# Reordering all five engines of a fused tokenizer, attention and channel-mix kernel, with other PSUM banks

## What is computed

```python
h = _L0_tok_ref(x, ln1_g, ln1_b, W, b, ln2_g, ln2_b)        # (64, 196, 256)
h = jnp.concatenate([h, txt], axis=1)                        # (64, 273, 256)
h = h + attn(_layernorm(h))
h = h + ffn(_layernorm(h))

# attn: heads attend to each other inside one token (the tensors are (n, s, head, d))
scores = jnp.einsum('nqhd,nkhd->nhqk', Q, K) * scale         # Q, K, V: 16 heads of 16
out = jnp.einsum('nhql,nlhd->nqhd', softmax(scores), V) @ Wo.T + bo
# ffn
x_prev = concatenate([zeros, x[:, :-1]]);  xr, xk = mixes of x and x_prev by mu_r, mu_k
r = sigmoid(xr @ W_r.T);  k = square(relu(xk @ W_k.T));  return r * (k @ W_v.T)
```

## Time and profile before

| | us |
|---|---|
| three runs | 1718.64, 1730.68, 1731.56 (median 1730.68) |
| the profiled execution, its time | 1723.9 |
| its span from first to last instruction | 1722.2 |
| TensorE busy | 1481.2 (86%) |
| VectorE busy | 1323.2 (77%) |
| ScalarE busy | 1260.7 (73%) |
| GpSimd busy | 933.9 (54%) |
| the DMA queue's packets, share of 16 engines | 72.5% |

### The profile page before, as it was taken

The page is one execution under the profiler, slowest core; times in us unless marked ns, Lnnn a source line. Parts: engine busy times, 40 slices in busy tenths (PEclk is TensorE's granted clock), DMA queues, the critical chain, the costliest instruction groups (busy, mean ns, idle before and its releaser), DMA issues.

```text
span 1722.2 us, 53654 instructions
## 1 busy us (share of the span) xinstructions
PE 1481.2 (86%) x18772; PEld 1404.6 (82%) x18772; DVE 1323.2 (77%) x3097; ACT 1260.7 (73%) x2401; POOL 933.9 (54%) x1508
## 2 busy tenths in 40 slices
PE   4686898989989899989989899998988988898866
PEld 4586798888888888888889888888988888888855
DVE  5666788787888787878878778887887878787642
ACT  2255787787788788777778877887877777786753
POOL 3121356556656555655655665565565556556547
PEclk8788899999999999999999999999999999999988
DMA  4267767877887876886697779788678877878651
GB/s 117 56 119 130 122 140 142 131 143 135 154 139 143 148 144 129 147 140 127 142 149 142 131 148 149 141 149 128 142 140 139 141 136 144 135 151 133 122 84 35
DMA packets 698051, 227.64 MB, mean 132 GB/s; under 512 B 612862, under 2 KB 669246, under 8 KB 697786
## 3 DMA queue, kind: packets, MB, share of 16 engines
q1 hardware_dynamic: 697786, 224.22, 72.5%
HBM read 121.64 MB, written 89.64 MB: 123 GB/s over the span
## 4 chain that ended last, share of the span: by engine, by line
PE 26%; SPq 21%; DMA 18%; ACT 10%; issue 10%; DVE 5%; POOL 1%; ACTq 0%; POOLq 0%; DVEq 0%
PE bank L976 13%; SPq L495 10%; DMA vd<-qkv_dram 7%; DMA on<-o_dram 5%; SPq L451 4%; PE bank L1050 3%; SPq L505 3%; ACT arena L873 3%; PE bank L1070 3%; DMA qk<-qkv_dram 3%; PE bank L1029 2%; ACT pt L883 2%; PE bank L1102 1%; DVE probs L732 1%; DMA o_dram<-probs 1%
## 5 line engine op out<-in xcount | busy, mean ns | idle before, releaser
L976 PE MATMUL bank<-wqkv,xnT 128*126 128x384 f32 (+1 forms) x1728 | 346.5, 345 | 3.7 <-issue 3.0
L1070 PE MATMUL bank<-wtok,xT 128*98 128x258 f32 x2304 | 311.7, 291 | 17.8 <-DVE xT L744 14.9
L1070 PEld LDWEIGHTS bank<-wtok,xT 128*98 128x98 f32 x2304 | 291.4, 171 | 22.7 <-DVE xT L744 19.7
L976 PEld LDWEIGHTS bank<-wqkv,xnT 128*126 128x126 f32 (+1 forms) x1728 | 293.4, 185 | 12.1 <-issue 6.2
L628 POOL TENSOR_TENSOR mixp<-mixf,mixp 128x364 fp32r<-128x364 f32 x192 | 186.3, 981 | 161.9 <-ACT mixp L950 159.9
L867 ACT ACTIVATE arena<-qk,ymask 128x768 f32<-128x768 f32 x192 | 165.5, 930 | 57.4 <-DMA qk<-qkv_dram 57.4
L873 ACT ACTIVATE arena<-vd,ymask 128x768 f32<-128x768 f32 x192 | 173.8, 958 | 23.4 <-DMA vd<-qkv_dram 23.4
L893 ACT ACTIVATE xcols<-xim 84x640 f32<-84x640 f32 (+1 forms) x192 | 131.8, 694 | 47.4 <-DMA xim<-in_x 47.1
L815 DVE TENSOR_TENSOR qkvt<-bank,bqkv 126x384 f32<-126x384 f32 (+1 forms) x288 | 154.0, 544 | 13.7 <-PE bank L976 12.1
L844 DVE SCALAR_TENSOR_TENSOR mixf<-dT,mus,zT 128x364 f32<-128x364 f32 x192 | 123.9, 666 | 36.2 <-POOL zT L622 31.3
L572 POOL TENSOR_TENSOR rs<-ve,small 126x3 f32<-126x3 f32 (+1 forms) x160 | 140.3, 877 | 12.5
(11 more groups left out here) (118 smaller groups left out, 3603.0 us busy)
## 6 DMA issues: line engine op xcount, KB each, us to landing
xim<-in_x SPq DMA_DIRECT2D x128, 294.0 KB
qk<-qkv_dram SPq DMA_DIRECT2D x48, 768.0 KB, 7.9
qkv_dram<-qkvt SPq DMA_DIRECT2D x96, 378.0 KB
vd<-qkv_dram SPq DMA_DIRECT2D x96, 192.0 KB, 7.2
...
```

What stands on the lines that cost most here:

```text
L976: ins = mm(psum, left(a, k), right(b, k), start=t == 0, stop=t == len(terms) - 1)
L1070: ins = mm(place("tok", c)[0:PT, 0:E + 2], xT[:, a, i0:i0 + GRID // 2, :].rearrange("p i w -> p (i w)"), wtok[:, b, ch, :], start=t == 0, ...
```

## The change

Two tables are replaced: `AT` (the order of all engines' operations) and `BANK` (the PSUM banks). `PE_ORDER`, all functions and all operations, shapes and transfers stay. The core of it, the rest of `AT` being changed in the same way:

```diff
-AT = dict(load=[0], xcols=[417, 674, 851], sq=[1995], ssq=[2418], sqm=[2869, 3373], x=[919, 1288, 1348], xh=[922,
-    1490, 1838], xl=[1354, 1898, 2141], tok=[2275, 3103], stat=[2780], statc=[3201], statr=[3205], rstd1=[3694],
+AT = dict(load=[0], xcols=[862, 903, 982], sq=[2421], ssq=[2671], sqm=[2859, 3630], x=[1152, 1176, 1586], xh=[1344,
+    1348, 2108], xl=[1754, 1816, 2421], tok=[2499, 3311], stat=[2811], statc=[3521], statr=[3556], rstd1=[3790],
...
-BANK = dict(x=[3, 6, 5], tok=[5, 6], stat=[3], xt=[7, 0], qkv=[1, 2, 7, 2, 0, 7], s=[0, 4], pt=[1, 4], av=[7, 4],
-    ont=[0, 1], wo=[1, 7, 4], zt=[4, 0], k=[2, 4], r=[2, 1, 7], val=[0, 2, 4])
+BANK = dict(x=[6, 7, 5], tok=[7, 5], stat=[6], xt=[4, 2], qkv=[2, 0, 3, 2, 1, 2], s=[1, 4], pt=[0, 4], av=[3, 0],
+    ont=[3, 0], wo=[0, 4, 2], zt=[4, 0], k=[1, 3], r=[3, 1, 2], val=[0, 4, 1])
```

More of the change, by code:

```diff
@@ L67 @@
-BANK = dict(x=[3, 6, 5], tok=[5, 6], stat=[3], xt=[7, 0], qkv=[1, 2, 7, 2, 0, 7], s=[0, 4], pt=[1, 4], av=[7, 4],
-    ont=[0, 1], wo=[1, 7, 4], zt=[4, 0], k=[2, 4], r=[2, 1, 7], val=[0, 2, 4])
+AT = dict(load=[0], xcols=[862, 903, 982], sq=[2421], ssq=[2671], sqm=[2859, 3630], x=[1152, 1176, 1586], xh=[1344,
+    1348, 2108], xl=[1754, 1816, 2421], tok=[2499, 3311], stat=[2811], statc=[3521], statr=[3556], rstd1=[3790],
+    txt=[7603], yn=[3988, 3990], st2=[4074, 4340], mv2=[4281, 5125], rstd2=[5480], hg=[5196, 6138], h=[6146, 6439],
+    hdma=[7328], st3=[10547, 10725, 10774], mv3=[10722, 10889, 11164], rstd3=[11189], xn=[11543, 11593, 11637],
+    xt=[11993, 12069], xnh=[12226, 12267], xnl=[12233, 12426], hb=[17201], qkv=[12732, 12904, 13448, 13478, 13833,
+    14478], qb=[12885, 13262, 13795, 13959, 14445, 14643], qkv_out=[13439, 14352, 14709], qk_in=[15517],
+    v_in=[16169], qplace=[16834, 17029], kspread=[16545, 16573, 16662, 16668], vspread=[17441, 17452, 17578, 17675],
+    s=[17227, 17306], mx=[17287, 17311], sub=[17413, 17451], exp=[17586, 17658], pt=[17621, 17683], ptc=[17768,
+    17789, 17806, 17826], av=[17916, 18038], rec=[18202, 18213], osb=[18205, 18272], o_out=[18677], o_in=[23238],
+    ont=[23784, 23907], onh=[23983, 23994], onl=[24107, 24118], wo=[24335, 24417, 25048], h2=[24815, 24874, 25219],
+    st4=[24847, 25809, 25844], mv4=[25923, 26026, 26032], rstd4=[26130], z=[26333, 26449, 26493], zt=[26708, 26736],
+    carry=[26680], ztc=[26869, 26978], d=[26930, 27140], edge=[27169], mix=[27427, 27437, 27818, 27896],
+    mixh=[27539, 27541, 28461, 30197], mixl=[27666, 27698, 30010, 30207], k=[28071, 28201], kr=[28456, 28494],
+    ksq=[28495, 28911], kah=[29188, 30265], kal=[30535, 30644], r=[30797, 30975, 31026], rt=[31217, 31279, 31394],
+    val=[31182, 31341, 31530], rv=[31519, 31729, 31748], add=[31914, 32129, 32140], out=[32355, 33356, 34358])
```

## The result

The changed kernel takes 1770.0 us (median, 1764.4 to 1780.3) where the kernel before takes 1727.2 us beside it: 1.026 of before, with a 95% interval of 1.020 to 1.033. The forecast was 1718 us, the range ended at 1750. It is slower by over 1%, for which the prediction gave 0.22, and not by the mechanism it had given that chance to.

What follows compares the result with a forecast made beforehand. It took TensorE's waits to be paced by the loop of transfers through SyncE's queue. Terms of -0.47 and -0.1 us over 16 quads gave -9.1 us; it wrote 1718 us, between 1715 and 1722, range 1688 to 1750.

Steps and rivals of the forecast that it cites:

- the mechanism it had given that chance to: Slot 3: `xcols` ahead of `z` wait for the image load, delaying `zt` and TensorE; 1739 to 1767 us, chance 0.22.
- the other waits: Waits at `s`, `pt`, the new banks and GpSimd's moved `hb` and `mixl`: 0 us for the time.
- The bank: New bank sharing, `wo`'s third piece after the first `qkv`: 0 us; if not, about 0.5 us each, 8 us in 16 quads.
- The clock: TensorE's granted clock, falling after long `ont` waits: up to 2 us a quad either way, in the range, not the forecast time.
- `av` in slot 1 no longer waits for `ptc`: Slot 1: the four `ptc` stand together, so the second half of `av` stops waiting: -0.47 us a quad.
- `zt` in slot 3: `z` ends 0.46 to 1.08 us later and `zt` with it; the wait at `ont` takes this up, 0.1 us left over.
- The sum: Slot 1's -0.47 and slot 3's -0.1 us a quad, times 16: -9.1 us, or -0.5%.
- The `pt` waits: TensorE's 12.8 us at `pt`, hanging on the v transfers: 0 us change.
- its work stays the same: No operation added or removed, so TensorE's work is unchanged and only waits can change.
- The tests: Signs in the changed profile: `av`, `ont`, `zt`, `pt`; wrong if `ont` leaves 50 to 100 us, new waits appear, or clock leaves 0.94 to 0.97.
- slower, by `z`: Rival: in slot 3 three `xcols` ahead of `z` wait for the image load; 1739 to 1767 us, chance 0.22.
- the sum's own term: Slot 3: `z` later by 0.46 to 1.08 us, of which 0.1 us a quad was taken as loss.

Runs made afterwards that it cites:

- experiment 2: The changed kernel with `hb` alone back at its old step (13522 for 17201): 1713.9 us, 0.994 of before.
- 6: The changed kernel with one more wait: `hb`, at its new place, starts only when both `qplace` copies of its chunk have ended: 1716.4 us, 0.994 of before.

## Why the prediction was wrong

**The step that failed** is the last sentence on the other waits: "`hb` a chunk later and `mixl` behind `ksq` move GpSimd's idle time only, since GpSimd is the least busy engine". The reason that I gave, that GpSimd is the least busy engine, does not bear on it. GpSimd's idle time did move; what I did not ask is under which VectorE instruction its work would then lie. The view for it was there: `hb` waited for `h2`, and so was kept clear of the copies by a wait that looked like waste. The effect itself stands in the trace of before as well: `hg` (L774), with two inputs in SBUF, takes 482 ns in the median there and up to 1546, and one copy took 1.69 us. The busy shares in the earlier trace rows (60.11 and 57.76 us in 100) can't show this, because both engines' work fits in the time, only not at the same moment. Experiments 2 and 6 set this step's price: 3.2 points of the time, 4.38 and 2.2 us for a copy of 0.56.

**The bank** was seen and its size was wrong. "`wo`'s third piece after the first `qkv` [...] the reader on VectorE stands in time by my count of the jobs between, so 0 us; if not, [...] about 0.5 us [...], 8 us in 16 quads." Measured: 3.22 us in slot 1 and 1.2 us in slot 2, 48.4 us in 1400. A count of jobs holds only as long as each has its own duration; the `qb` came late as one job ahead of it took eight times as long. With the copies clear, the same bank costs 10.0 us in 1400, 0.52 us a piece in slot 1: this is the size that I had written. A second new bank wait was not in the prediction: the second `k` piece takes bank 3 behind `ont` and waits for `onl` to read it, 9.3 us in 1400 in the changed kernel and 13.0 in experiment 2, and none before. No run took it out.

**The clock** was named as a lever for `ont`, and it was pulled elsewhere. The prediction had at most 2 us a quad of it. In slot 1 the new wait puts TensorE at its lower level behind it, which makes the six `wo` and ten `x` matmuls 0.36 + 0.71 = 1.07 us longer, and `s` 0.5 us more.

**Right, seen in the changed kernel:** `av` in slot 1 no longer waits for `ptc`. `zt` in slot 3 waits 1.84 us for `z` (1.3 to 2 forecast), and `ont` behind it does not wait any more:

```profile
1186.98 0.85 PE L1116 MATMUL bank<-ident,on 126*128 126x126 f32 x6 [1.84 <-ACT on L933]
```

**The sum,** with `hb` set aside: 0.994 in experiments 2 and 6 against 0.995 forecast. This is less of a hit than it looks. The `pt` waits (12.8 us), which I had left standing, went; `s` fell from 16.3 to 10.3, `ont` from 81.4 to 72.0; on the other side `zt` rose from 11.5 to 26.2, and the waits of `wo` for `qb` (10.0 us) and of `k` for `onl` (13.0 us) came. All waits of TensorE from 200 to 1600 us sum up to 141.2 us before and 137.4 in experiment 2, whose 1400 us hold 1% more matmuls (16649 for 16488). Terms of both signs were missed that nearly cancel, so that the sum is near is luck. Over the whole span of experiment 2 TensorE is idle 10.6 us less and busy 3.4 us less; that its work stays the same, as the prediction had it, is nearly so.

**The tests** named at the end of the prediction did their work: "I am wrong if TensorE waits at a place that it did not wait at before (`wo` or `x` for VectorE: a bank)", and the clock left its 0.94 to 0.97 by a thousandth. `ont` was to stay at 80 us and is 66.5; some 3 us of the difference is that the same 1400 us hold fewer quads (13.6 for 14.1), and the rest was not predicted. The rival "slower, by `z`" did not come: `zt`'s wait grew by 1.03 us a quad, inside the sum's own term.

What stays open: why the length of GpSimd's next operation lets a copy in or not in slot 1, and what else decides it at other places; and whether bank 3 and the other place of `txt` give the 0.3% and 0.4% that they seem to.
